# Nine stored blocks per sequence, query work by quarters, paced block loads, and row gathers issued five at a time

## The reference, cut to what matters

```python
x = x + L0(x, weights[cond])                 # bct,bcd->bdt
x = x + L1(x, W, A[adapter], Bm[adapter])    # dense plus a low-rank part
# L2, on x:
q = rope(rms(x @ Wq.T), pos); k = rope(rms(x @ Wk.T), pos); v = x @ Wv.T
slot, off = pos // 16, pos % 16
k_blocks = k_blocks.at[block_tables[slot], :, off, :].set(k)   # v alike
scores = q @ k_all.T * SCALE                 # k_all: all blocks of the table
allowed = (kpos <= pos) & (kpos > pos - 128)
x = x + softmax(where(allowed, scores, -inf)) @ v_all @ Wo.T
x = x + L3(x, W3[expert], b3[expert])
```

## Time and profile before

| what | us |
|---|---|
| median of 3 runs | 148.35 |
| lowest, highest | 147.51, 148.99 |
| the profiled execution | 145.84 |
| its span in the trace | 143.8 |
| PE, DVE, ACT, POOL busy | 122.3, 95.8, 93.0, 75.1 |
| first `scores` | 62.15 |
| data moved | 32.56 MB |

### The profile page before, as it was taken

The page is one execution under the profiler, slowest core; times in us unless marked ns, Lnnn a source line. Parts: engine busy times, 40 slices in busy tenths (PEclk is TensorE's granted clock), DMA queues, the critical chain, the costliest instruction groups (busy, mean ns, idle before and its releaser), DMA issues.

```text
span 143.8 us, 4133 instructions
## 1 busy us (share of the span) xinstructions
PE 122.3 (85%) x1366; PEld 85.4 (59%) x1366; DVE 95.8 (67%) x370; ACT 93.0 (65%) x288; POOL 75.1 (52%) x109
## 2 busy tenths in 40 slices
PE   0019999899979967879799999999999999999972
PEld 0008985787858955344344576767667665756650
DVE  0589914397976698049975487787788879796321
ACT  0046959618997693755677987879888777854200
POOL 1857773000000487779988889798788714041000
PEclk9999999999999997799999999999999999999999
DMA  3993699999499122339997964787777775546561
GB/s 91 272 348 105 182 431 426 351 426 417 185 433 352 28 81 92 109 113 378 328 281 255 267 181 113 242 243 193 236 227 219 206 218 176 147 144 186 146 191 36
DMA packets 21726, 32.56 MB, mean 226 GB/s; under 512 B 5162, under 2 KB 18730, under 8 KB 20682
## 3 DMA queue, kind: packets, MB, share of 16 engines
q1 hardware_dynamic: 15536, 19.76, 41.3%
q0 software_dynamic: 2960, 11.67, 24.0%
q10 hardware_dynamic: 3210, 0.87, 2.9%
HBM read 23.91 MB, written 8.39 MB: 225 GB/s over the span
## 4 chain that ended last, share of the span: by engine, by line
PE 78%; DVE 7%; ACT 5%; DMA 4%; SPq 3%; issue 2%; DVEq 0%
PE bank L1164 9%; PE bank L1180 7%; PE bank L1045 6%; PE bank L1221 6%; PE bank L1234 6%; PE bank L1197 6%; PE bank L1055 5%; DMA nat<-in_L_cond_Wv 4%; PE bank L1229 4%; PE bank L994 3%; PE bank L1208 3%; PE bank L1068 3%; PE bank L1142 2%; PE bank L1046 2%; PE bank L1002 2%; PE bank L1029 2%
## 5 line engine op out<-in xcount | busy, mean ns | idle before, releaser
L692 ACT ACTIVATE pr<-S,nb 128x160 f32<-128x160 f32 x64 | 27.1, 431 | 2.8 <-DVE nb L935 2.8
L935 DVE CUSTOM_DVE_ANT_0 S<-bank,mask 128x160 f32<-128x160 f32 x64 | 18.0, 317 | 10.0 <-PE bank L1164 9.5
L924 DVE TENSOR_SCALAR pr<-pr,ri 128x128 f32<-128x128 f32 x64 | 21.2, 376 | 1.1
L475 POOL DMA_INDIRECT kvA<-kv_rows,rowA x16 | 18.4, 1149 | 4.3 <-issue 4.3
L463 POOL DMA_INDIRECT kvB<-kv_rows,rowB x4 | 4.3, 1085 | 26.3 <-DMA kv_rows<-kvn 25.6
L502 POOL TENSOR_TENSOR prB<-pr,ri 128x64 f32<-128x64 f32 x32 | 9.6, 299 | 16.0 <-DVE ri L920 15.9
L1164 PE MATMUL bank<-KT,QT 32*64 32x160 f32 x256 | 16.3, 319 | 1.8 <-ACT KT L662 1.0
L475 POOL DMA_INDIRECT blkp<-kv_rows,rowA x16 | 15.9, 993 | 3.0 <-issue 2.2
L676 ACT COPY PTA<-bank 128x256 f32<-128x256 f32 x32 | 11.8, 369 | 5.2 <-PE bank L1180 5.2
L1180 PE MATMUL bank<-cst,pr 128*128 128x128 f32 x64 | 13.1, 285 | 0.2
L692 ACT ACTIVATION_READ_ACCUMULATOR pr<-S,nb 128x1 f32 x64 | 12.7, 198 | 0.0
(11 more groups left out here) (204 smaller groups left out, 283.9 us busy)
## 6 DMA issues: line engine op xcount, KB each, us to landing
We<-in_L_cond_W SPq DMA_DIRECT2D x16, 256.0 KB, 3.6
kvn<-in_L_cond_W SPq DMA_DIRECT2D x16, 256.0 KB, 3.6
kv_rows<-blkp SPq DMA_DIRECT2D x1, 2048.0 KB, 12.7
kv_rows<-blk SPq DMA_DIRECT2D x1, 2048.0 KB, 6.4
kv_rows<-blkp SPq DMA_DIRECT2D x4, 512.0 KB, 4.6
xin<-in_x SPq DMA_DIRECT2D x2, 512.0 KB, 7.0
kv_rows<-kvn SPq DMA_DIRECT2D x2, 512.0 KB, 5.4
be<-in_L_cond_b SPq DMA_DIRECT2D x32, 32.0 KB
```

The source lines that it names most:

```text
L475: pool.indirect_dma_start(out=kvA(b, slice(0, 2 * KV)), out_offset=None, in_=written(b), in_offset=bass.IndirectOffsetOnAxis(ap=rowA[:, b: ...
L692: act.activation(pr[:, n // B4 % 2, u, n % B4, :], S[:, n % 2, u, :], ACT.Exp, bias=nb[:, n % 4, u:u + 1], scale=-1.0, accum_out=rs[:, n % ...
L924: ts(e_, e_, ri[:, n % 8, u:u + 1], None, ALU.mult).then_inc(s_pn, 1)
L935: dve.tensor_tensor_reduce(S[:, n % 2, u, :], bank[2 + (2 * n + u) % 3][:, 0:KEYS], mask[:, n, :], -SCALE, 3e38, ALU.add, ALU.min, nb[:, n ...
```

## The change

- **Nine blocks.** Only the first 9 blocks of a window are loaded and written (`PB`), so the third unit has 32 blocks instead of 128, and a sequence b lies in unit `(9b+8)//128`. For the other two blocks of a window only the table entries are read: the new rows that fall into them are still found through `hit`, which now has the stored blocks first (`place`).
- **Paced loads.** Load i waits until load i-2 has landed. POOL's `hi` and `wo_s` work, which follows, waits with it.
- **Queries by quarters.** `q_part` has four parts of two tiles. The sums of all four, the whole of the first, and BY_ROOT and COS of the second lie before the loop; the rest is in steps 0, 1, 4 to 7 and 8 to 11 (`Q_PARTS`), after `normalise`. `turn_q(1)` moves from before the loop to step 2.
- **Order.** ACT's prologue is reordered: `permute(2)` and `(3)` after `keep_kv(0)`, the distances in pairs, `keep(6..8)` before `keep_qn(2)`, `permute(5)` and `root_q(2)` before `keep_qn(3)`. PE does the last transposes of weights ahead of `project_q(0)` instead of behind `project_q(1)`. DVE does `k_part[1]` before `rowA` and `rowB`.
- **Gathers.** After the first 8 sequences POOL issues sequences 8 to 11 at step 0, 12 to 15 at step 2, and then the four of group g+3, with their `gather_b`, in one go at step 4g+2, behind `prB` of sequence 4g.

```diff
-AHEAD = 10
+GATHERED = {0: 3 * B4, **{4 * g + 2: (g + 4) * B4 for g in range(NT - 3)}}
...
+def place(f):
+
+    return divmod(f, PB) if f < STORED else (lambda b, j: (b, PB + j))(*divmod(f - STORED, WB - PB))
+
+
+def unit_blocks(u):
+
+    return min(P, STORED - u * P)
...
-        UNIT_OF = [(b * WB + WB - 1) // P for b in range(B)]
-        Q_BANK, Q_STEP = (5, 6, 1, 1), (11, 15)
+        UNIT_OF = [(b * PB + PB - 1) // P for b in range(B)]
+        Q_BANK, Q_STEP = (5, 6, 1, 1), (2, 11, 15)
...
             def load_blocks(i):
                 u, kv = LOADS[i]
+                if i >= 2:
+                    pool.wait_ge(s_bl[i - 2], 16)
                 pool.wait_ge(s_tab[u], 16)
...
-                while nxt < min(B, n + AHEAD):
+                while nxt < min(B, GATHERED.get(n, 0)):
                     gather_a(nxt)
                     nxt += 1
...
             keep_kv(0)
+            permute(2)
+            permute(3)
             keep_kv(1)
-            permute(2)
+            act.wait_ge(s_cst0, 16)
+            act.wait_ge(s_hi, 1)
+            for j in (0, 1):
+                distance(0, j)
             root_k(0)
             keep_kv(2)
-            permute(3)
+            for j in (2, 3):
+                distance(0, j)
             keep_kv(3)
-            act.wait_ge(s_cst0, 16)
-            distances(0)
+            root_k(1)
             keep(5, WqT[:, :, :, :].rearrange("p k s c -> p k (s c)"), square(0))
             keep(5, BQ[:, :], bank[5][:, 0:D])
-            root_k(1)
             permute(4)
...
+            keep_qn(0)
+            for j in (0, 1):
+                distance(1, j)
+            root_q(0)
+            for j in (2, 3):
+                distance(1, j)
+            keep_qn(1)
+            keep(6, W1T[:, :, :], square(1))
+            keep(7, BT[:, :], bank[2][:, 0:D])
+            keep(8, WoT[:, :, :], bank[3][:, :].rearrange("p (c o) -> p c o", c=2))
+            root_q(1)
+            keep_qn(2)
+            permute(5)
+            root_q(2)
+            keep_qn(3)
+            keep_q(0)
+            root_q(3)
+
+            act.activation(warm[:, 1:2], eps[:, 0:1], ACT.Exp)
...
-            keep_q(0)
-            keep_q(1)
+            keep_ka(0)
             keep_x2(0)
-            keep_ka(0)
             keep_kb(0)
...
-            q_part = [norm_rotate(0, h, H, q_heads(h), q_sq(h), q_cos(h), q_sin(h), ssq, rstd, 4 * h + 4, s_qn, s_qsin, s_qready)
-                      for h in range(2)]
+            q_part = [norm_rotate(0, i, 2 * i, 2, H, q_heads(i), q_sq(i), q_cos, q_sin, ssq, rstd, s_qn, s_qsin, s_qready)
+                      for i in range(4)]
             SUMS, BY_ROOT, COS, SIN, ADD = range(5)
+            Q_PARTS = {0: (8,), 1: (9,), **{3 + k: (10 + k,) for k in range(1, 5)}, **{7 + k: (15 + k,) for k in range(1, 5)}}
...
             for part in (SUMS, BY_ROOT, COS, SIN, ADD):
                 q_part[0][part]()
             masks(0)
-            q_part[1][SUMS]()
-
+            for i in (1, 2, 3):
+                q_part[i][SUMS]()
+            for part in (BY_ROOT, COS):
+                q_part[1][part]()
             masks(1)
...
-                if 1 <= n <= 4:
-                    q_part[1][n]()
+                for part in Q_PARTS.get(n, ()):
+                    q_part[part // 5][part % 5]()
...
-            project_q(0)
-            project_q(1)
             pe.wait_ge(s_kvk, NT)
             turn_square(1, nat, 0, [])
...
             i_.then_inc(s_wt, 1)
+            project_q(0)
+            project_q(1)
             project_q(2)
             project_q(3)
...
             turn_q(0)
-            turn_q(1)
             layer1(0)
```

More of the change, by code:

```diff
@@ L54 @@
 WROWS = WB * BLOCK
+PB = 9
+UROWS = PB * BLOCK
 NU = 3
 FLAT = B * WB
+STORED = B * PB
 NW = 3
@@ L60 @@
 WIN0 = NEW0 + B * T
-NROWS = WIN0 + NU * P * BLOCK
+NROWS = WIN0 + B * UROWS
 BIG = 1e30
@@ L105, in __init__ @@
             "later": c([[i < q for i in range(NWI)] for q in p]),
-            "win_row": c([[WIN0 + q * WROWS + x + 1 for x in range(WROWS)] for q in p]),
+            "win_row": c([[WIN0 + q * UROWS + x % UROWS + 1 for x in range(WROWS)] for q in p]),
             "adapter": c(p // RANK),
@@ L450, in _ @@
             landed = [0]
-            written = lambda b: kv_rows[0:WIN0 + (UNIT_OF[b] + 1) * P * BLOCK, :]
+            written = lambda b: kv_rows[0:min(NROWS, WIN0 + (UNIT_OF[b] + 1) * P * BLOCK), :]
             def windows(b):
@@ L614, in _ @@
             keep_kv(0)
+            permute(2)
+            permute(3)
             keep_kv(1)
-            permute(2)
+            act.wait_ge(s_cst0, 16)
+            act.wait_ge(s_hi, 1)
+            for j in (0, 1):
+                distance(0, j)
             root_k(0)
             keep_kv(2)
-            permute(3)
+            for j in (2, 3):
+                distance(0, j)
             keep_kv(3)
-            act.wait_ge(s_cst0, 16)
-            distances(0)
+            root_k(1)
             keep(5, WqT[:, :, :, :].rearrange("p k s c -> p k (s c)"), square(0))
             keep(5, BQ[:, :], bank[5][:, 0:D])
-            root_k(1)
             permute(4)
[L627 to L634, removed]
-            keep_qn(2)
-            keep_qn(3)
-            root_q(1)
-            act.activation(warm[:, 1:2], eps[:, 0:1], ACT.Exp)
             def keep_q(i):
@@ L701, in _ @@
                 if n in Q_STEP:
-                    keep_q(2 + Q_STEP.index(n))
+                    keep_q(1 + Q_STEP.index(n))
                 g = n // B4 + 2
@@ L900, in _ @@
                 k_part[0][part]()
+            for part in (SUMS, BY_ROOT, COS, SIN, ADD):
+                k_part[1][part]()
             dve.wait_ge(s_rowT, 1)
@@ L905, in _ @@
                    1.0, None, ALU.subtract).then_inc(s_rowi, 1)
-            for part in (SUMS, BY_ROOT, COS, SIN, ADD):
-                k_part[1][part]()
             rotations(0)
@@ L1136, in turn_ka @@
                 for i, n in enumerate(Q_STEP):
-                    if g == n // B4 + 2:
-                        pe.wait_ge(s_qt, 2 * (i + 3))
+                    if i and g == n // B4 + 2:
+                        pe.wait_ge(s_qt, 2 * (i + 2))
                 for j in range(B4):
@@ L1253, in _ @@
                 if n in Q_STEP:
-                    pe.wait_ge(s_ktb, n // B4 + 2)
-                    turn_q(2 + Q_STEP.index(n))
+                    if n != Q_STEP[0]:
+                        pe.wait_ge(s_ktb, n // B4 + 2)
+                    turn_q(1 + Q_STEP.index(n))
                 if 0 <= n - TURN < B:
```

67 lines of the change are left out of this document (36 added, 31 removed).

## The result

The changed kernel took 150.11 to 155.95 us in four runs, median 153.02; the kernel before took 148.31 us in the same job. The ratio of the comparable runs is 1.026, interval 1.016 to 1.035: slower, by 3.8 us at that ratio, though the interval leaves open whether by more than 2%. The forecast was 148.7 us in a range that ended at 150.7, so the median lies outside it; the likeliest outcome had been a time within 1% or so of the kernel before (chance 0.52), and slower by more had 0.25. The profiled execution took 150.11 us, span 148.3, against 145.84 and 143.8 before: 4.5 us more in the span.

The account below looks back on a forecast made before the run. PE was taken to bound the loop, and DVE's first half of the queries the chain before it. A gain of 0.8 us and a loss of 1.1 made +0.3 on 148.35: 148.7 us, range 146.3 to 150.7.

Parts of the forecast that it names:

- Before the loop: Prologue: first quarter ready at 49.45, `layer1(0)` at 55.3 instead of 56.24, with ACT as the bound; 0.8 us gained.
- rival 3: Before the loop: the low clock covers all of `layer1(0)`, costing 1.5 us, 150.2 us in all; chance 0.1.
- The clock: At `layer1(0)`: PE's wait brings the 1.2 GHz level as before, the same 1.25 us loss, possibly differing between runs.
- Loads, pacing, windows: Block loads and window writes: nine blocks and pacing were costed at 0 on the path, up to 0.5 us if late.
- The quarters in the loop: DVE in steps 8 to 12: the fourth quarter's 3.23 us makes scores late and PE wait, 1.1 us lost.
- the spare time: DVE in a group of loop steps: 1.98 us to spare, set against the quarter's extra 3.23 us.
- The burst costs nothing: POOL at steps 4g+2: five gathers in one go are the same work as when spread, so cost nothing.
- 1.7 us of slack: POOL behind a burst: the `prB` are done at 94.6 and PE comes for them at 96.27.
- Rival 2: POOL becomes the loop's bound when gathers in a burst, some held by DVE, take over 1.3 us; 150.5 us, chance 0.15.

Follow-up runs that it names:

- f1: The changed kernel itself, run again with all its parts; 150.74 us against 147.06 for the kernel before, ratio 1.023.
- f2: The changed kernel with gathers one a step instead of in bursts; 148.48 us, 1.007 of the kernel before.
- i2: f2 with DVE's order alone changed, no quarter's work in steps 8 to 11; 146.61 us against 147.66 for the kernel before, 0.991.
- f3: f2 with POOL holding VBD and three `prB` of a group back to its last step; 153.61 us, 1.048 of the kernel before.
- f4: f2 with i2's DVE order and ACT keeping the third and fourth quarter earlier, `permute(5)` behind `root_q(3)`; 147.63 us against 147.06 for the kernel before.
- i4: i2 with ACT's order changed too and `permute(5)` behind the first keys; 145.94 us against 147.66 for the kernel before, 0.988.
- jobs f and i: Two measuring jobs holding the runs lettered f and i, on chips where the kernel before has a median of 147 to 148 us.
- i1: The kernel before with the gathers in bursts and nothing else changed; 149.84 us against 147.66, ratio 1.013.
- i3: The kernel before with nine blocks and paced block loads alone; 147.62 us against 147.66, ratio 0.999.

## Why the prediction was wrong

**Before the loop: right.** `layer1(0)` at 55.29 (said 55.3), first quarter ready at 49.67 (49.45), ACT's order as worked out. Of the 0.8 us gain 0.5 arrived, since `layer1(0)` lay almost wholly in the low clock (3.62 us, instead of 3.16 by the chain or 3.36 by the timeline): rival 3's event, at 0.3 to 0.5 us of its 1.5.

**The clock: right for the profiled execution, a missing term for the median.** Said to stay as it was; in the profiled execution it did. In two of the four executions it did not: 155.29 and 155.95 us at a mean clock of 0.967, about 5 us above the other two, for which the sum had no term. They put the median above the range; without them the time, 150.4, would have been inside it, and the forecast of about no change would have looked better than its working was. Runs of the other kernels with the quarters show the same level: one of four in f1, three of ten in f2, two of ten in i2, all four in f3 (0.966 and 0.967), none in f4 and i4 (0.976 to 0.987). None of the runs of the kernel before in the jobs f and i, of i1 and of i3 is below 0.986. That PE's longer pause before `layer1(0)` brings it is not shown.

That the loss would differ from run to run, as the prediction took it from the Trainium skill (TensorE: Matmul & The Clock Gate, What's actually happening), agrees with the runs: the ten executions of i2 have a mean granted clock of 1.0 once, 0.988 seven times and 0.965 or 0.966 twice. So does i2 against f2: the same wait of 2.95 us, and 1.95 us instead of 3.6 for the four matmuls.

**Loads, pacing, windows: right.** i3 prices them at nothing.

**The quarters in the loop: right in kind, under-sized.** The sum gave 1.1 us for steps 8 to 12. f2 needs 10.8 us from S(8) to S(12) (82.08 to 92.91) where before needed 8.3 (80.54 to 88.88), 2.5 more; 0.9 comes back in the four steps behind, though the prediction saw no pause of PE to get it back in; 1.1 us more, not priced at all, is lost ahead of S(8), by the pieces in steps 0 and 4 to 7, where I had taken PE to be covered. By the times i2 and f2 put it at 1.65%, 2.4 us. The failed term is the spare time: of 1.72 us in which DVE was idle from S(8) to S(12) only 0.66 took up work, the rest stayed waiting for PE. And I added the pieces to DVE's durations of the trace before, but a shifted DVE meets POOL's VBD elsewhere, and 0.6 became 1.35 us.

**The burst costs nothing: wrong, and the main step that failed.** The working asked what POOL's queue holds up, and who waits for `prB`: nobody did, with 1.7 us of slack, and nobody does. In the trace after, the gathers of the bursts from step 2 on take 0.94 to 1.09 us and PE does not wait for POOL. What I did not ask is what POOL's instructions do to the engine beside them. The operations moved were equal in number and length, so I called it the same work; but their place against DVE's scalings had been part of the kernel's speed. 1.25% alone (i1), 1.6% on top of the quarters.

**Rival 2** had the right pair of engines and, for this loss, the wrong direction. It let DVE hold the gathers up, to above 1.3 us each. That does happen: in the kernel before, gathers that began within 0.3 us of the start of a query product of 1.22 us took 1.75 to 1.96 us (49.80, 64.66, 66.71), and in the changed kernel, whose products are half as long, one took 1.39 (62.88). But the bursts from step 2 on escape it, and there POOL holds DVE up. The sentence of the Trainium skill that the rival drew on (SBUF — State Buffer, Who interferes with whom) states an exclusion that works both ways, and the earlier trace rows had VBD at 96.07 with its 1.05 us. A scaling that meets VBD can be held for its 1.05 us, a tail more and the end of the gather ahead, up to 1.97 instead of 0.28 us in i1, against a spare of 1.98 us of DVE in a group: a term of the sum whose least size, VBD's own length, was within reach.

The two terms add: 1.25% for the burst (i1) and 0.7% for the rest (f2) make 1.95%, f1 measured 2.3% (interval 1.0 to 3.6).

## What to carry to other kernels

When an instruction list is regrouped on GpSimd, write down for each of its tensor operations what VectorE does at that moment before and after, not only who waits for its result: a pair of scalings of 0.6 us or a mask of 0.5 us took 1.4 to 2.2 us beside the end of a gather, a 1 us operation of GpSimd and the short ones behind it. Slack that the windows view shows as idle time on an engine is slack only for work that doesn't move the rest against its neighbours. And of a change with several parts the parts may well pull apart: here the quarters with DVE's pieces set elsewhere and the gathers left alone give 0.991 of the time, 0.988 with ACT's order mended too, where the whole gave 1.026.

## What was not expected of the hardware

- The same program takes 147 to 148 us (medians) on some chips and 168 to 172 on others, with pauses of all engines at once, up to 5.9 us, which the traces put down to "issue" or "remote". Bursts of gathers cost 1.25% on the one kind and 7.4 to 8.2% on the other.
- The low clock's place moves. An earlier `layer1(0)` (54.8 in f4) escaped it, and `layer1(1)` got it instead: 6.5 us and more at the low level in i4, 3.78 us for four matmuls that take 1.98 at the high one. In the changed kernel the runs of 155 to 156 us have a mean clock of 0.967, nearly f3's 0.966, whose trace shows just such a second stretch; that it is the same one is an inference, since no trace of those runs exists.
